# Three more seven-product Q steps, and the output-weight reload moved from SyncE's to ScalarE's queue

## The reference

```python
Q = (layernorm(x) @ Wq.T)         # 32 heads of 128, in 8 groups of 4
K, V = ctx @ Wk.T, ctx @ Wv.T     # 8 heads of 128, one for each group
scores = Q K^T * 128**-0.5, causal, softmax
x = x + tanh(g_xattn) * (softmax(scores) @ V) @ Wd.T
x = x + tanh(g_ffn) * (layernorm(x) @ dequantize(qweight).T + bias)
```

## Time and profile before

| | us |
|---|---|
| median of three timed runs | 1046.54 |
| the profiled execution | 1045.23 |
| its span | 1043.4 |
| PE busy | 1006.0 (96%) |
| DVE busy | 720.3 (69%) |
| ACT busy | 500.3 (48%) |
| POOL busy | 290.2 (28%) |

### The profile page before, as it was taken

One profiled execution on the slowest core, in us unless ns is written; L12 is line 12 of the kernel. 1 busy time (PEld: TensorE's weight loads), 2 busy tenths in 40 slices (PEclk: granted clock), 3 DMA queues, 4 the chain that ended last, 5 costly groups with the idle time before them and its releaser, 6 DMA issues.

```text
span 1043.4 us, 21305 instructions
## 1 busy us (share of the span) xinstructions
PE 1006.0 (96%) x8130; PEld 597.5 (57%) x8130; DVE 720.3 (69%) x1484; ACT 500.3 (48%) x1033; POOL 290.2 (28%) x287
## 2 busy tenths in 40 slices
PE   5889999999999999999999999999999999999996
PEld 3455555555555555455555555555567776767752
DVE  6856777777586676865667667565667767666678
ACT  5777676675633343334543434334444444444422
POOL 1355665465714001412210503143000120000004
PEclk9999999999999999999999999999999999999998
DMA  7748546534474542455544775146754444543211
GB/s 281 229 150 289 204 160 203 163 101 169 130 258 139 155 92 102 157 157 177 207 172 162 237 212 176 26 162 181 216 162 149 158 130 148 180 140 138 91 42 60
DMA packets 97523, 168.65 MB, mean 162 GB/s; under 512 B 35472, under 2 KB 68240, under 8 KB 83728
## 3 DMA queue, kind: packets, MB, share of 16 engines
q1 hardware_dynamic: 97424, 167.30, 49.6%
HBM read 110.89 MB, written 33.55 MB: 138 GB/s over the span
## 4 chain that ended last, share of the span: by engine, by line
PE 84%; DVE 10%; ACT 3%; issue 2%; DMA 1%; SPq 0%; DVEq 0%; ACTq 0%
PE pa L1715 33%; PE py L1715 30%; PE av L1894 5%; PE pa L1790 4%; PE av L1790 3%; PE pp L1872 3%; PE ps L1856 2%; PE pp L1856 2%; DVE q L1214 2%; PE py L1954 1%; DVE sc L1310 1%; DVE row_max L1308 1%; DVE sc L1304 1%; DVE sc L1321 1%; DMA raw_q<-in_wqT 1%
## 5 line engine op out<-in xcount | busy, mean ns | idle before, releaser
L1715 PE MATMUL py<-wd,att 128*128 128x512 f16 x1488 | 337.6, 379 | 1.7 <-DVE att L1334 0.9
L1715 PE MATMUL pa<-xT,wq 128*128 128x512 f16 x1152 | 257.2, 379 | 10.1 <-DVE q L1214 7.8
L1715 PEld LDWEIGHTS py<-wd,att 128*128 128x128 f16 x1488 | 143.1, 98 | 158.6 <-issue 2.8
L1715 PEld LDWEIGHTS pa<-xT,wq 128*128 128x128 f16 x1152 | 109.3, 98 | 145.2 <-issue 19.3
L1343 DVE SCALAR_TENSOR_TENSOR xacc<-py,f_y,xacc 128x512 f32<-128x512 f32 x128 | 95.7, 747 | 91.4 <-PE py L1715 91.3
L939 ACT ACTIVATE att<-av 128x256 f16<-128x256 f32 x256 | 80.8, 385 | 135.9 <-PE av L1894 135.4
L1334 DVE SCALAR_TENSOR_TENSOR att<-av,att 128x256 f16<-128x256 f32 x256 | 93.5, 418 | 65.6 <-ACT att L939 65.3
L888 ACT ACTIVATE q<-pa 128x512 f16<-128x512 f32 x96 | 56.7, 591 | 171.0 <-PE pa L1715 171.0
L1715 PE MATMUL pa<-wv,cT 128*128 128x128 f16 x1536 | 96.2, 219 | 0.0
L1715 PEld LDWEIGHTS pa<-wv,cT 128*128 128x128 f16 x1536 | 89.8, 98 | 0.9
L1214 DVE SCALAR_TENSOR_TENSOR q<-pa,q 128x512 f16<-128x512 f32 x96 | 65.8, 686 | 35.2 <-ACT q L888 33.5
(11 more groups left out here) (180 smaller groups left out, 1396.8 us busy)
## 6 DMA issues: line engine op xcount, KB each, us to landing
wq<-kept_q SPq DMA_DIRECT2D x24, 1024.0 KB, 8.7
wd<-kept_d SPq DMA_DIRECT2D x23, 1024.0 KB, 6.8
v_dup<-v_nat SPq DMA_DIRECT2D x128, 128.0 KB, 2.4
raw_d<-in_wdT SPq DMA_DIRECT2D x8, 1024.0 KB, 10.3
kept_q<-wq SPq DMA_DIRECT2D x8, 1024.0 KB, 9.0
kept_d<-wd SPq DMA_DIRECT2D x8, 1024.0 KB, 5.6
raw_d<-in_wqT SPq DMA_DIRECT2D x8, 1024.0 KB, 7.1
raw_q<-in_wqT SPq DMA_DIRECT2D x7, 1024.0 KB, 5.5
```

The lines of the kernel that those rows point to most:

```text
L1715: last = pe.matmul(out, stationary(a, i), moving(b, i), start=(i == 0 and (a, b) == PASSES[0]), stop=(i == count - 1 and (a, b) == PASSES[ ...
```

## The change

`FIRST_FAST` becomes 21: Q of steps 21, 22 and 23 (the last three groups of block 2) is computed by seven half products too, in steps n = 20, 21 and 22. With it `deferred` holds from n = 19 on in place of 22. Block 2 now also needs mixed tokens: they are made at step 12 and transposed at steps 14 and 15, into the first half of `raw_q`; those of block 3 go into the first half of `raw_d`. The mixed weights must be ready earlier, so the mixing that was in step 21 is now in step 10, and the groups are mixed in another order (`MIX_ORDER` starts at group 5). Mixed weights are read back three more times. Last, `back_d` of a step with `fast(n + 1)` (steps 20 to 30) is no longer issued by SP but by ACT, behind `hi_22(m, 1)`.

```diff
-            "p (c k n) -> p c k n", c=2, k=KC) for raw in (raw_q, raw_q)]
+            "p (c k n) -> p c k n", c=2, k=KC) for raw in (raw_q, raw_d.rearrange("p c h (k n) -> p c h k n", k=KC))]
...
-        FIRST_FAST = 3 * GROUPS
+        FIRST_FAST = 2 * GROUPS + 5
...
-        MIX_STEPS = (7, 12, 13, 14, 15, 17, 18, 21)
+        MIX_STEPS = (7, 10, 12, 13, 14, 15, 17, 18)
...
-                sp.wait_ge(wq_lo, HPG * GROUPS)
+                if tb == 2:
+                    sp.wait_ge(wq_lo, HPG * GROUPS)
+                else:
+                    sp.wait_ge(s_lo, HPG * GROUPS)
...
-                    if one is some[FEW - 1] and fast(n + 1) and n < LAST:
-                        back_d(n)
-                if not some and fast(n + 1) and n < LAST:
-                    back_d(n)
...
-                sp.wait_ge(s_kept[m % 2], 16 * GROUPS // 2)
+                for par in range(2):
+                    sp.wait_ge(s_kept[par], 16 * GROUPS // 2)
...
+            def back_d(n):
+
+                act.wait_ge(y_mm, 4 * n)
+                act.wait_ge(d_kept, 16 * GROUPS)
+                act.dma_start(wd[:, :, :, :].rearrange("p c h n -> p (c h n)"), kept_d[n % GROUPS]).then_inc(d_back, 16)
...
                     hi_22(m, 1)
+                    back_d(n)
                     hi_12(m, 1)
```

More of the change, by code:

```diff
@@ L358, in transposes @@
                     if NORMS[call][0] == 2 or not fast(GROUPS * NORMS[call][1]) or t < 2 or i >= 2]
-        EARLY, FEW = 6, 5
+        EARLY = 6
         MIXED = ([(t, c, i) for t in (2, 3) for c in (HI, LO) for i in range(KC)]
```

## The result

The changed kernel took 1050.37 us, the median of 17 runs (1046.84 to 1057.32), against 1046.53 for the kernel before (17 runs, 1045.04 to 1049.62). The ratio is 1.0042, with a 95% interval of 1.0029 to 1.0055: slower, where I had forecast 1046.4 and no difference. The profiled execution took 1050.18 us with a span of 1048.4, so it is close to the median. The spread has grown too, from 4.6 us to 10.5.

A forecast was written before the change was run, and what follows sets the result against it. PE, busy 96% of the span, was taken to bound the kernel. The terms -4.55 + 2.7 + 1.0 + 0 + 0.3 + 0.4 = -0.15 us gave a predicted median of 1046.4, range 1044.4 to 1048.6 (chance 0.60).

The forecast's parts named there:

- The saving: Steps 19 to 22: PE's own work falls from 123.28 to 118.73 us, 4.55 saved, with step 19 at 32.15.
- VectorE in step 20: Step 20: VectorE, late from step 19's zero-point operations, makes PE wait at `run(m, 0, 7)` and `run(m, 0, 4)`: +2.7 us.
- the output weights: First y tile of steps 20 to 22: `wd` lands up to 1.1 us late beside SP's traffic; +1.0 together.
- the 1.1 that I had named as the sign of being wrong: Any step: the forecast is wrong if `wd` costs over 1.1 us in a step.
- The sentence that nothing large is in flight in steps 23 to 30: Steps 23 to 30: weights come at the step's start, so the `wd` load is covered: 0.
- The rival with late loads: First y tile of steps 20 to 22: `wd` lands late; 1053.5 us at landings of 10.1, 1050.2 at 9.0; chance 0.17.
- The small terms: Step 21 at `copy_p1` +0.3 us, step 11 after the moved mixing +0.4, mixed tokens in steps 12 to 15 0.
- the 0.4: Step 11: mixing moved to step 10 keeps VectorE busy longer, so the FFN product and third Q head wait: +0.4 us.
- `copy_p1`: Early step 21: ScalarE finishes block 3's high parts of mixed tokens after this copy is wanted: +0.3 us.
- the transposes for block 3: Before `run(24, 0, 4)`: margin of 1.9 us; no wait expected given the other losses, so 0.
- the cap of 3.5: Before `run(24, 0, 4)`: block 3's transposes on SP let at most 3.5 us of the gain come through.

The follow-up runs named there:

- the best kernel: Changed kernel with step 19's zero-point work and GpSimd's FFN additions earlier, and the weight readbacks of steps 22, 23 and 24 moved: 1041.67 us, ratio 0.9961.
- the queue-only kernel: The kernel before with only the output-weight load of fast steps 23 to 30 moved from SyncE's to ScalarE's queue: 1046.18 us, ratio 0.9996.
- the best kernel's variant with more moves: The 1041.67 us kernel with the feed-forward operations moved forward in step 11 as well: 1043.81 us, ratio 0.9985.

## Why the prediction was wrong

- **The saving was right.** Step 19 was to take 32.15 and took 32.13; with every wait gone a fast step takes 28.86 or 28.87 in steps 20 to 22, and steps 19 to 22 sum to 118.74 us in the best kernel, against the 118.73 worked out.
- **VectorE in step 20 was right in mechanism and place, and small by 0.9.** Measured 2.03 + 1.53 = 3.56 against 2.7, inside the bounds of 1.5 to 4.0. The scores came 0.93 us later than reckoned, which is about the difference: I had taken the remaining zero-point operations at 0.9, 1.0 and 1.2, as if partly held, and in the changed order all of them fall beside GpSimd's `ln_lo`, at 1.33 each. The sum looked at `ffn_add` only. I had weighed "Who interferes with whom" of the page "SBUF — State Buffer" in the Trainium skill against one row and gone by the row; the rule that two-input operations of the two engines exclude each other is nearer to what came. Two such operations took 2.89 us beside GpSimd's additions and 0.75 without them, and moving the additions away brought step 20 from 30.71 to 28.86 us.
- **The step that failed is the output weights: "I take 0.3 a step, +1.0 together".** They cost 2.34, 0.69 and 0, in sum 3.03. (Three times 0.3 is 0.9, not 1.0; that is the smallest part of it.) The wait of 2.34 is over the 1.1 that I had named as the sign of being wrong. My likely landing was 7 to 8.5 us, and it was 10.1, 8.4 and 5.9. I had read the 10.1 of the earlier trace rows as the worst case and the 7.2 of the earlier trace rows as the nearest. What I didn't look at is how far ahead of the load the batch was issued. In step 26 of the kernel before it was the same 2.5 MB, begun 9.0 us ahead of the load at 864.38:

```profile
855.43 0.55 SPq L436 DMA_DIRECT2D wq<-kept_q  x1
```

In step 20 after the change it is 5.4 us. The term went by the size of the traffic and left its distance out. The runs show what the distance does: 7.8 to 11.9 us where the batch began 1.7 to 6.3 us ahead, 5.1 to 7.3 where it was about 8 or more. The sentence that nothing large is in flight in steps 23 to 30 passed over that batch too. The rival with late loads had the right mechanism, and 0.17 was too little for it. Its 1050.2 for a landing of 9.0 is next to the measured 1050.37 by luck: it takes 1.6 us in each of three steps and 2.7 for VectorE, neither of which came. The Trainium skill says in "DMA: Bandwidth & Descriptors", section "Issuing engines are not separate DMA queues", that DMAs from different engines run on the same 16 DMA engines; the kernels with only the queue changed agree, with 0.9996 where no batch is near, and waits of 2.51 and 2.34 us in step 20 from either queue.

- **The clock had no term at all.** Where PE waited 2.85 to 4.55 us for the load, four profiles show the next twelve y products at 4.37 to 5.30 us instead of 2.75, with the granted clock at or near 0.50. In the profiled execution of the changed kernel the wait was 2.34 and no drop followed, so its steps 19 to 22 sum to only 2.5 us more than before, while the medians differ by 3.8. Among its 17 executions the five slowest, from 1052.96 us up, have a mean granted clock of 0.992 to 0.994 and the three fastest one of 0.996 or 0.997, but the fourth fastest, 1048.41, has 0.994 too; the 12 of the queue-only kernel all stay at 0.996 to 0.998. That such drops make up the remaining 1.3 us and the wide spread is likely and not shown, since only one execution has a trace. The 2.5 us alone would have left the forecast's range of 1044.4 to 1048.6.
- **The small terms.** Step 11 grew by 0.31 and step 12 shrank by 0.30, so the 0.4 came to nothing; `copy_p1` cost nothing instead of 0.3; the transposes for block 3 cost nothing, as forecast, also in the best kernel, where PE runs 4.5 us earlier and the cap of 3.5 that I had set didn't show.

By terms, then, for steps 19 to 22: -4.54, VectorE 3.56, output weights 3.03, and 0.44 left over, mostly in gaps of step 20 under half a microsecond, make +2.49. For the same steps I had summed to -0.55, and to -0.15 with the 0.4 of step 11. Of the 3.0 us between, 2.0 are the output weights and 0.9 VectorE. What stays open is the share of the clock in the median, why the best kernel's variant with more moves spreads over 9 us, and the unexplained 2.52 us in its profile. The 1041.67 rests on six runs, of which the slowest took 1045.87 at a mean clock of 0.995.

## What to carry to other kernels

When a step gets shorter, list every load whose issue is tied to the shortened step and every large batch that isn't, and look how far apart they now are; a landing time read where nothing else flies is no price for a meeting. Take a cure for the first wait of a step only together with what is late next. Here each cure of VectorE's waits was given back as long as a batch was near: without the batch moved, at the load of the same step, and with only the first batch moved, at that of the next. Moving the first batch alone kept its gain. And of two kinds of fix, a faster queue and a different moment, it was the moment that mattered here.

## What was unexpected of the hardware

- In steps 20 to 22 of the changed kernel and of those made from it with the batch whole, the 1 MB of output weights took 7.8 to 11.9 us in the eight cases in which the issue of the 2.5 MB had begun 1.7 to 6.3 us ahead. They took 5.1 to 7.3 where it had begun about 8 us or more ahead, or wasn't ahead at all. Issued earlier into such a meeting, they landed hardly earlier.
- The DMA engines were busy and moved little at the end of such a meeting: share 1.31 with 136 GB/s and 1.16 with 48 GB/s in the windows above, where the windows ahead of it had a share of 0.94 to 1.07 with 316 to 425 GB/s. The transposes alone don't do that: SyncE went on issuing them until 716.9 us, and from 703 us on the share was 0.16 with 33 GB/s. What kept the engines busy in between isn't shown.
- A wait of 2.85 us in a kernel whose PE is busy 96% of the time was followed by 5.30 us for twelve products that take 2.75, so it cost nearly twice its length; waits of 2.34 and 2.51 in two others were followed by 2.76.
